# The last head of a graph attention layer reordered: copies ahead of normalisations, a tile finished one iteration sooner, output rows stored in two parts

## The reference

```
q, k, v = x@Wq+bq, x@Wk+bk, x@Wv+bv          # x after a first layer norm; 4 heads of 512
alpha   = q[dst].k[src] / sqrt(512); softmax over the edges of each dst
agg     = sum over edges of softmax * v[src]
h       = (agg + x@Wskip + bskip) @ Wlin + blin + ...
h       = x + gamma*(h - mean)/sqrt(var + eps) + beta      # "h" norm and residual
z       = (h - mean)/sqrt(var + eps)                       # "z" norm
# small logic MLP on z: 16-bit one-hot fields decoded to nibbles, three MLPs (and/or/xor)
#   of hidden width 160 for a low and a high nibble, one of them selected by flags,
#   result added as a one-hot of 32 columns at z[:, 80:112]
out     = h + z'
```

## Time and profile before

| | |
|---|---|
| median of 3 runs | 1184.33 us (1184.18 to 1184.88) |
| profiled execution, its own time | 1184.66 us |
| its span | 1182.5 us |
| PE busy | 1094.7 us, 93% of the span |
| DVE, ACT, POOL busy | 599.4, 329.4, 171.8 us |
| last head, first score maximum to the end | 951.2 to 1182.5 us |

### The profile page before, as it was taken

How to read it: one execution, slowest core, us unless ns; L and a number is a source line. 1 busy time by engine, 2 the same in 40 slices (tenths; PEclk the granted TensorE clock), 3 DMA queues, 4 the chain that set the end, 5 groups by cost and what they waited for, 6 DMA issues and landing times.

```text
span 1182.5 us, 14807 instructions
## 1 busy us (share of the span) xinstructions
PE 1094.7 (93%) x5666; PEld 896.2 (76%) x5666; DVE 599.4 (51%) x1534; ACT 329.4 (28%) x512; POOL 171.8 (15%) x292
## 2 busy tenths in 40 slices
PE   3789899999999999999999999999999999998861
PEld 2566666677888888888888888888888888877750
DVE  6788788835234333324334332433443234666776
ACT  3353424230233132213222221322232132233210
POOL 4222422220000000000000000000000002534555
PEclk9899899999999999999999999999999999999985
DMA  6534435423001001000100100100010000000101
GB/s 229 166 125 146 139 129 194 165 92 144 1 1 72 1 1 72 1 2 12 61 1 1 72 1 2 32 40 1 1 72 1 1 14 31 18 18 19 35 29 42
DMA packets 13653, 64.41 MB, mean 54 GB/s; under 512 B 1387, under 2 KB 1780, under 8 KB 10001
## 3 DMA queue, kind: packets, MB, share of 16 engines
q1 hardware_dynamic: 8977, 46.67, 11.6%
q0 software_dynamic: 4608, 16.78, 3.8%
HBM read 44.11 MB, written 19.34 MB: 54 GB/s over the span
## 4 chain that ended last, share of the span: by engine, by line
PE 64%; DVE 17%; issue 8%; ACT 5%; DMA 3%; POOL 2%; SPq 0%; POOLq 0%; DVEq 0%; ACTq 0%
PE ps_o L1056 7%; PE ps_o L1057 7%; PE ps_o L1058 7%; PE ps_r L1056 6%; PE ps_r L1057 6%; PE ps_r L1058 6%; PE ps_s L1056 5%; PE ps_s L1058 5%; PE ps_s L1057 5%; DMA acc<-in_x 3%; DVE onehot_src L685 3%; PE ps_t L1261 3%; PE ps_s L1140 2%; DVE opnd_lo L674 1%; DVE prob L1028 1%
## 5 line engine op out<-in xcount | busy, mean ns | idle before, releaser
L1056 PE MATMUL ps_s<-xT_hi,tT 128*128 128x512 f32 (+1 forms) x480 | 175.5, 366 | 0.3 <-DVE top L1013 0.3
L1058 PE MATMUL ps_s<-xT_hi,tT 128*128 128x512 f32 (+1 forms) x480 | 170.1, 354 | 0.0
L1057 PE MATMUL ps_s<-xT_lo,tT 128*128 128x512 f32 (+1 forms) x480 | 169.6, 353 | 0.0
L1056 PE MATMUL ps_o<-y,pT 128*128 128x512 f32 (+1 forms) x400 | 157.8, 394 | 0.0
L1057 PE MATMUL ps_o<-y,pT 128*128 128x512 f32 (+1 forms) x400 | 157.2, 393 | 0.0
L1058 PE MATMUL ps_o<-y,pT 128*128 128x512 f32 (+1 forms) x400 | 157.0, 392 | 0.0
L639 ACT ACTIVATE prob<-prob,nbias 125x1250 f32<-125x1250 f32 x40 | 53.7, 1342 | 255.3 <-DVE nbias L1021 255.3
L1013 DVE CUSTOM_DVE_ANT_0 prob<-ps_s,maskb 125x1250 f32<-125x1250 f32 x40 | 58.2, 1456 | 119.0 <-issue 119.0
L594 ACT ACTIVATE pT<-ps_t 128x500 fp32r<-128x500 f32 (+1 forms) x120 | 58.0, 519 | 203.3 <-PE ps_t L1261 203.3
L879 DVE TENSOR_TENSOR pT<-ps_t,pT 128x500 fp32r<-128x500 f32 (+1 forms) x120 | 67.3, 590 | 93.1 <-ACT pT L594 93.1
L453 POOL MEMSET row_mask<- 18x1 f32 x1 | 0.1, 88 | 709.8 <-DMA xz<-in_mlp_w 709.8
(11 more groups left out here) (244 smaller groups left out, 1977.0 us busy)
## 6 DMA issues: line engine op xcount, KB each, us to landing
products<-prod_parts POOLq DMA_DIRECT2D x32, 512.0 KB, 4.1
gbuf<-products SPq DMA_DIRECT2D x4, 2048.0 KB, 7.8
mbuf<-products SPq DMA_DIRECT2D x4, 2048.0 KB, 7.8
stage<-in_Wq SPq DMA_DIRECT2D x4, 1024.0 KB, 7.9
stage<-in_Wk SPq DMA_DIRECT2D x4, 1024.0 KB, 5.7
stage<-in_Wskip SPq DMA_DIRECT2D x4, 1024.0 KB, 6.2
stage<-in_Wv SPq DMA_DIRECT2D x3, 1024.0 KB, 4.9
stage<-in_Wlin SPq DMA_DIRECT2D x3, 1024.0 KB, 4.7
```

The source lines that it names most:

```text
L1056: nc.tensor.matmul(out_, a[0], b[0], start=start, stop=False)
L1057: nc.tensor.matmul(out_, a[0], b[1], start=False, stop=False)
L1058: return nc.tensor.matmul(out_, a[1], b[0], start=False, stop=stop)
```

## The change

Only the last head and its tail change; no arithmetic is left out.

- ACT: `tail_result` at the head of an iteration is gone. z of tile d-3 is normalised in `tail_mid`, after exp and mask of tile d and before the side copies; h of tile d-2 stays at the end (`tail_end`).
- DVE: `results(d-4)` and `features(d-3)` stand at the end of iteration d, behind `add_out(d-2)`, the moments of h of tile d-2 (now ahead of `pt_low` of blocks 0, 1) and that `pt_low`. `feat_copy(d-4)` stands at the head of the iteration, the moments of z of tile d-3 behind the bias. `results` has one small operation more and adds its 32 columns to acc itself.
- PE: for 4 <= d < NT the transposes of the features of tile d-4, with their wait for `feat_ready`, stand between the two parts of the scores of tile d, and the hidden products of that tile ahead of `outputs(d-2)`; from d = NT on both are at the end.
- POOL: z's factors first, then residual plus beta, `choice(k-3)`, the final sum of tile k-3 without columns 80 to 111 in two pieces of 400 and 80 columns (`add_rows`), then h's factors, gamma, residual. `row_factors` has three operations in place of four.
- SP: each tile is stored as columns from 112 on (two transfers) and, after `z_final`, columns 0 to 111 (two transfers): 40 stores in place of 10.
- The loops end at NT+3 = 13 on PE and DVE in place of 15.

```diff
--- before.py
+++ after.py
@@ -57,6 +57,8 @@
 FEAT = 6
 ROUND = 12582912.0
 LO_HI_OUT = 80
+HOT_END = LO_HI_OUT + 32
+ROW_CUTS = [(0, 112), (112, R - 112)]
 
 G_PROD, M_PROD, K_PROD = range(3)
@@ -293,10 +295,10 @@
             for t in range(NT - 2):
                 fill[last, "y", t] = t
             c = NT - 2
-            for k in range(NT + 6):
-                if last and 0 <= k - 5 < NT:
-                    fill[last, "hid", k - 5] = c
-                    c += 2
+            for k in range(NT + 4):
+                if last and 0 <= k - 4 < NT:
+                    fill[last, "feat", k - 4] = c
+                    c += 1
                 if k % 2 and k < NT - 1:
                     fill[last, "t", k] = c
                     c += 2
@@ -304,8 +306,8 @@
                     fill[last, "y", NT - 2 + k] = c
                     c += 1
                 if last and 0 <= k - 4 < NT:
-                    fill[last, "feat", k - 4] = c
-                    c += 1
+                    fill[last, "hid", k - 4] = c
+                    c += 2
 
         LAST_Y = fill[False, "y", NT - 1]
 
@@ -371,10 +373,16 @@
                     sp.dma_start(xres[0:R, :], x[R * t:R * t + R, :]).then_inc(xres_in, 16)
                 if t >= 4:
                     done = t - 4
-                    sp.wait_ge(o_ready, done + 1)
-                    sp.dma_start(out[R * done:R * done + R, :],
-                                 acc[0:R, done, :]).then_inc(out_done, 16)
-            sp.wait_ge(out_done, 16 * NT)
+                    sp.wait_ge(o_ready, 2 * done + 1)
+                    for a, w in ROW_CUTS:
+                        sp.dma_start(out[R * done + a:R * done + a + w, HOT_END:],
+                                     acc[a:a + w, done, HOT_END:]).then_inc(out_done, 16)
+                    sp.wait_ge(o_ready, 2 * done + 2)
+                    sp.wait_ge(z_final, done + 1)
+                    for a, w in ROW_CUTS:
+                        sp.dma_start(out[R * done + a:R * done + a + w, 0:HOT_END],
+                                     acc[a:a + w, done, 0:HOT_END]).then_inc(out_done, 16)
+            sp.wait_ge(out_done, 16 * NT * 2 * len(ROW_CUTS))
 
         @block.gpsimd
         def _(pool):
@@ -475,24 +483,32 @@
                 link(nc.gpsimd.tensor_scalar(s_act, s_act, 1.0, None, ALU.add))
                 nc.gpsimd.tensor_tensor(gate, s_act, gate, ALU.mult).then_inc(gate_ready, 1)
 
-            for k in range(2, NT + 5):
-                if 0 <= k - 4 < NT:
...
+            def row_factors(t, ready):
+
+                link(nc.gpsimd.tensor_scalar(veps[0:R, t:t + 1], mv[0:R, t, 1:2], EPS, None, ALU.add))
+                link(nc.gpsimd.tensor_tensor(rstd[0:R, t:t + 1], veps[0:R, t:t + 1], eps_pow[0:R, t:t + 1], ALU.pow))
+                nc.gpsimd.tensor_scalar(nmr[0:R, t:t + 1], mv[0:R, t, 0:1], rstd[0:R, t:t + 1], -1.0,
+                                        ALU.mult, ALU.mult).then_inc(ready, 1)
+
+            def add_rows(t):
+
+                for a, b in ((HOT_END, D), (0, LO_HI_OUT)):
+                    nc.gpsimd.tensor_tensor(acc[0:R, t, a:b], xz[t % RESULTS][0:R, a:b], acc[0:R, t, a:b],
                                             ALU.add).then_inc(o_ready, 1)
+
+            for k in range(2, NT + 3):
+                if 0 <= k - 3 < NT:
+                    pool.wait_ge(z_var, k - 2)
+                    row_factors(k - 3, z_rstd)
                 if k - 2 < NT:
                     pool.wait_ge(xres_in, 16 * (k - 1))
                     link(nc.gpsimd.tensor_tensor(xres[0:R, :], xres[0:R, :], beta_bc[0:R, :], ALU.add))
+                if 0 <= k - 3 < NT:
+                    choice(k - 3)
+                    add_rows(k - 3)
+                if k - 2 < NT:
                     pool.wait_ge(h_var, k - 1)
-                    factors(slice(k - 2, k - 1), h_rstd)
-                if 0 <= k - 3 < NT:
-                    pool.wait_ge(z_var, k - 2)
-                    factors(slice(k - 3, k - 2), z_rstd)
-                if k - 2 < NT:
+                    row_factors(k - 2, h_rstd)
                     a = acc[0:R, k - 2, :]
                     pool.wait_ge(h_norm, k - 1)
                     link(nc.gpsimd.tensor_tensor(a, a, gamma_bc[0:R, :], ALU.mult))
@@ -595,21 +611,22 @@
                                          ps_t[:, (3 * d + j) % 2, 0:w * R].rearrange("p (k r) -> p k r", k=w),
                                          ACT.Copy).then_inc(pt_hi, 1)
 
-            def tail(k):
+            def tail_mid(k):
+
+                if 0 <= k - 3 < NT:
+                    t = k - 3
+                    act.wait_ge(z_rstd, t + 1)
+                    if t >= RESULTS:
+                        act.wait_ge(o_ready, 2 * (t - RESULTS + 1))
+                        act.wait_ge(z_final, t - RESULTS + 1)
+                    normed(xz[t % RESULTS][0:R, :], t, z_norm)
+
+            def tail_end(k):
 
                 if 0 <= k - 2 < NT:
                     t = k - 2
                     act.wait_ge(h_rstd, t + 1)
                     normed(acc[0:R, t, :], t, h_norm)
-
-            def tail_result(k):
...
 
             def normed(dst, t, ready):
                 nc.scalar.activation(dst, acc[0:R, t, :], ACT.Identity, scale=rstd[0:R, t:t + 1],
@@ -628,10 +645,8 @@
             def head(h, last):
                 for t in range(NT - 2):
                     rotating_hi(h, t, "y", t)
-                for d in range(NT + 4 if last else NT + 2):
+                for d in range(NT + 3 if last else NT + 2):
                     n = NT * h + d
-                    if last:
-                        tail_result(d)
                     if 0 <= d - 2 < NT:
                         pt_high(h, d - 2, [2])
                     if d < NT:
@@ -641,6 +656,8 @@
                         if not (last and d == NT - 1):
                             act.wait_ge(top_ready, n + 2)
                             mask((d + 1) % NT)
+                    if last:
+                        tail_mid(d)
                     if not last and d == NT:
                         take_g0(h + 1)
                     for local, g, half in side_fills(last, d):
@@ -650,7 +667,7 @@
                     if 0 <= d - 1 < NT:
                         pt_high(h, d - 1, [0, 1])
                     if last:
-                        tail(d)
+                        tail_end(d)
 
             with act.Fori(0, H - 1) as h:
                 head(h, False)
@@ -978,33 +995,29 @@
                     ins = nc.vector.tensor_scalar(s_one[:, r, :], nib_id[0:R, :], s_sel[:, r:r + 1],
                                                   s_gate[t % 2], ALU.is_equal, ALU.mult)
                 chain(ins)
-                o = z[0:R, LO_HI_OUT:LO_HI_OUT + 32]
-                nc.vector.tensor_tensor(o, o, hot, ALU.add).then_inc(z_final, 1)
...
+                chain(nc.vector.tensor_tensor(hot, z[0:R, LO_HI_OUT:HOT_END], hot, ALU.add))
+                o = acc[0:R, t, LO_HI_OUT:HOT_END]
+                nc.vector.tensor_tensor(o, hot, o, ALU.add).then_inc(z_final, 1)
+
+            def z_moments(t):
+                dve.wait_ge(h_res, t + 1)
+                moments(t, acc[0:R, t, :], z_var)
+
+            def h_moments(t):
+                dve.wait_ge(acc_ready, NT * H + t + 1)
+                moments(t, acc[0:R, t, :], h_var)
 
             for half in range(2):
                 rotating_lo(0, half - 2, "t", (0, half, 0))
             def head(h, last):
                 for t in range(NT - 2):
                     rotating_lo(h, t, "y", t, last)
-                for d in range(NT + 6 if last else NT + 2):
+                for d in range(NT + 4 if last else NT + 2):
                     n = NT * h + d
                     if 0 <= d - 2 < NT:
                         pt_low(h, d - 2, [2])
-                    if last and 0 <= d - 5 < NT:
-                        results(d - 5)
-                    if last and 0 <= d - 4 < NT:
-                        features(d - 4)
+                    if last and 0 <= d - 4 and d < NT:
+                        feat_copy(d - 4)
                     if d < NT:
 
                         dve.wait_ge(scores_done, n + 1)
@@ -1020,6 +1033,8 @@
                         dve.wait_ge(shift_ready, n + 1)
                         nc.vector.tensor_scalar(nbias[0:R, d:d + 1], cd_col(h, d), shift[0:R, d:d + 1],
                                                 SCALE, ALU.subtract, ALU.mult).then_inc(nbias_ready, 1)
+                    if last and 0 <= d - 3 < NT:
+                        z_moments(d - 3)
                     for local, g, half in side_fills(last, d):
                         rotating_lo(h, local, "t", (g, half, h if g else h + 1), last)
                     if d < NT:
@@ -1038,10 +1053,17 @@
                         rotating_lo(h, fill[last, "y", NT - 2 + d], "y", NT - 2 + d, last)
                     if 2 <= d < NT + 2:
                         add_out(h, d - 2)
+                        if last:
+                            h_moments(d - 2)
```

(79 more changed lines are left out.)

## The result

The changed kernel takes 1219.3 us (4 runs, 1218.38 to 1220.18) against 1184.26 us (4 runs) for the kernel before: ratio 1.0294, 95% interval 1.0282 to 1.0306, 2.9% slower. The forecast was 1218 us. The profiled execution of the changed kernel took 1220.18 us, its span is 1218.5 us.

What follows compares the result with a forecast made beforehand. PE, with gaps, was taken to bound the last head, a DVE, POOL and ACT chain its tail. The walk's 1203.0 plus 13.5 of half clock, 2.2 around the span, less 0.3, gave 1218 us; eight in ten 1199 to 1229.

Steps and rivals of the forecast that it cites:

- The wait and the loop: PE needs features at T + 3.6 us (T: output products' end), DVE has them at T + 10.0; this closes a loop.
- POOL over DVE's small operations: In DVE's results, POOL's gamma and residual hold the small operations, costing 1.7 us.
- the narrower reading: Only operations seen held in the trace are held; six-column ones at T + 4.4 pass, features about T + 9.1 us.
- Even windows: Even iterations, from one end of PE's output products to the next: 22.05 us, plus 2.3 for the clock.
- Odd windows: Odd iterations with side products, between ends of output products: 29.6 us, plus 2.3 for the clock; sign 27 to 32.
- the clock's term: PE's half clock behind its wait: 2.3 us in each of five iterations, 2 for iterations 10 and 11, 13.5 together.
- the walk: Sum of iteration times from T(3) = 1005.20 to the end at 1203.0 us, without the half clock.
- Iterations 10 and 11: From T(9) = 1147.7 to T(11) = 1173.3 us, plus 2 us for the clock.
- The tail: From T(11) to the end: 25.2 us of chain and 4.5 for the last store, 29.7 against 33.3 before.
- Rivals 1 and 2: PE's clock stays up, 1204.5 us, 12%; POOL is not in DVE's way, 1204 us, 10%; both together 1190.
- rival 3: PE's wait is covered if features reach it within 3.6 us of T; DVE's load binds, 1170 us, 7%.
- Small gaps are not enough: PE's clock in iteration 7 stayed at 1.00 with 4.2 us idle in several pieces, so small gaps cause no fall.

Runs made afterwards that it cites:

- e1: Changed kernel with DVE's features of tile d-3 ahead of add_out(d-2) for d < 10, one-hot in its own buffer: 1179.6 us, ratio 0.9955 to the kernel before.
- e4: Changed kernel with PE's feature transposes behind scores and side products, hidden products behind output products, DVE's feature copy just ahead of add_out: 1180.3 us.
- e2: Changed kernel with POOL's gamma and residual on 32 of 512 columns, the other 480 left out: 1203.5 us.
- e3: Changed kernel with 24 extra matmuls of 512 columns in PE's wait ahead of the feature transposes, iterations 5 to 9: 1206.5 us.
- e7: Changed kernel with each tile stored whole, in one transfer, behind z_final and both sums: 1221.4 us.
- e9: Kernel of e6 with PE's hidden products of tile d-4 behind the output products for 4 <= d < 10: 1167.6 us, ratio 0.9851 to the kernel before.
- e5: Kernel before with only ACT's copy of block 2 of the transposed probabilities put ahead of z's normalisation in the last head: 1180.1 us.
- e6: Kernel of e1 with, on ACT, z's normalisation behind the two side copies instead of ahead: 1175.2 us.
- e8: Changed kernel with h's moments at the end of DVE's iteration, behind results and features, for d < 10: 1211.2 us.

## Why the prediction was right, step by step

- *The wait and the loop*: right. Features at T + 10.0 were forecast, the transposes began 9.6 to 10.7 us behind T, after idle times of 5.75 to 6.82 us (4.6 to 6.7 forecast), and e1 and e4 opened the loop from either side.
- *POOL over DVE's small operations*: right in kind and size, 1.7 forecast, 1.7 by e2 on the mean. Which operations are held depends on where POOL stands: in iterations 6 and 8, where its gamma starts 4.0 us behind T and not 4.7, the six-column product passes at 0.17 us, and the addition before it takes 0.64 and an operation of two columns 0.92 (1061.69 and 1062.76); hence 9.6 there and 10.3 to 10.7 elsewhere. The wider rule, which the Trainium skill gives in SBUF — State Buffer, "Who interferes with whom", is now shown for the six-column product (1.19 us beside POOL, 0.19 in e2 without it); the narrower reading would have given T + 9.1.
- *Even windows*: 22.05 + 2.3 against 24.3 to 24.5. *Odd windows*: 29.6 + 2.3 = 31.9 against 33.8, which is also beyond the 27 to 32 that were named as a sign: the clock's term was too small. The clock fell twice, behind the long wait and again behind the waits of 1.3 and 1.5 us for the side copies (output products 8.7 us in place of 7.0); the forecast counted one fall. By e3 the clock costs 3.7 and 3.4 us in the odd windows and 14.3 us in all five, where 11.5 stood; the walk itself was 0.5 and 0.8 us short in the odd windows (30.1 and 30.4 against 29.6).
- *Iterations 10 and 11*: 25.6 us and 2 for the clock forecast, 25.6 measured. The clock's part costs nothing in iteration 10: in e3 it is 12.6 us at a clock of 0.97 and here 12.2 at 0.86. That DVE's lateness hides it is the likely reason; no run isolates it.
- *The tail*: 29.7 forecast, 28.8 measured. Two terms were off, in opposite ways: the last store, 4.5 us forecast, where the span ends 2.2 us behind its issue (e7 puts the split at 2.3 us), and the chain ahead of it, 25.2 us forecast and 26.6 measured.
- T(4) came at 1023.3 and not 1022.35. The misses (+0.9 up to T(4), +4.0 in iterations 5 to 9, -2.0, -0.9) partly cancel, to 2.0 us of span; that the median came within 1.3 us of the forecast is luck on top of a right mechanism.
- Rivals 1 and 2 are each a real part (e3, e2) and neither a case by itself. Of rival 3 the condition failed in this kernel. e1 meets it by another order and gains 0.45% (1179.6 us, not the 1170 of the rival); with the two further moves of e9 it is 1167.6: an order of this kind can beat the old one.
- "Small gaps are not enough" for a fall of the clock was too wide a rule, read from one window. It holds there (a wait of 2.05 us at 1065.80, clock 1.00 behind it) and fails in the changed kernel, e1 and e5.

## What to carry to other kernels

When a program moves work behind a wait, ask at which point another engine needs the result and where that engine stands then: here 10 us of work stood behind the end of PE's products, wanted 3.6 us after it, and every later product queued behind that. Such a loop can be opened from either side, by having the producer do it in idle time ahead of its wait or the consumer ask for it later, and one look at both timelines from the same event shows it. The stalls of the matrix engine cost their length here, and then 14.3 us of half clock behind them.

## What the runs showed of the hardware that was not expected

- PE's granted clock fell behind waits as short as 1.3 to 2.0 us in a stretch that was otherwise busy (iterations 5 and 7 of the changed kernel and of e1, iteration 5 of e6 and of e8), and did not behind others of that length: 2.05 us in iteration 7 of the kernel before, 1.31 in iteration 7 of e8, 1.27 and 1.31 in e3, where the long wait before had been filled. Which of two equal waits is followed by a fall was not settled.
- The lock between DVE and POOL goes the other way too: a POOL operation of one column took 1.29 us in the changed kernel (L484 at 1048.03) while DVE's pass over the probabilities (L1043, 1047.83, 1.45 us) ran; earlier, at 1024.28, without that pass, it took 0.19.
